# Semaphores of a stage cleared inside the next stage, one barrier at each seam, last attention stores awaited where they are loaded

## The reference

```
xn = layernorm(x)
s  = attention0(xn)              # 16 heads of 16, full softmax, output projection, + b_o + xn
g  = silu(ffn0(xn))              # router, 8 experts of rank 64, cumulative sums over tokens, two branches
x  = x + s * g
xn = layernorm(x)
s  = attention1(xn)              # same heads, |i - j| <= 64 only, output projection, + b_out
g  = silu(ffn1(xn))              # base matrix + 8 gated LoRA experts of rank 16
x  = x + s * g
```

## Time and profile before

| | us |
|---|---|
| median of three runs | 2464.88 |
| the profiled execution, its own time | 2465.71 |
| its span (first to last instruction) | 2464.1 |
| outside of the span | 1.6 |
| PE busy | 2221.7 (90%) |
| DVE busy | 1840.2 (75%) |
| ACT busy | 1448.4 (59%) |
| POOL busy | 462.4 (19%) |
| mean granted TensorE clock, share of full | 0.948 |

### The profile page before, as it was taken

How to read it: one execution, slowest core, us unless ns; L and a number is a source line. 1 busy time by engine, 2 the same in 40 slices (tenths; PEclk the granted TensorE clock), 3 DMA queues, 4 the chain that set the end, 5 groups by cost and what they waited for, 6 DMA issues and landing times. The chain is left out here.

```text
span 2464.1 us, 44375 instructions
## 1 busy us (share of the span) xinstructions
PE 2221.7 (90%) x14912; PEld 1240.2 (50%) x14912; DVE 1840.2 (75%) x3240; ACT 1448.4 (59%) x2165; POOL 462.4 (19%) x673
## 2 busy tenths in 40 slices
PE   7786899999999999999999999987999986899988
PEld 4564333333333333333333333326888875666688
DVE  5553889999999999999999999922443466798746
ACT  4443177777777777777777777771222222375643
POOL 0000000000000000000000000003555520365645
PEclk8998599999999999999999999999999999597999
DMA  6776700220500500502304002006567459766564
GB/s 208 260 246 191 94 4 6 40 29 3 63 6 8 61 3 12 57 5 32 36 6 56 13 5 63 3 5 173 153 181 167 121 211 361 152 151 138 146 166 129
DMA packets 189121, 231.80 MB, mean 94 GB/s; under 512 B 72720, under 2 KB 122768, under 8 KB 186064
## 3 DMA queue, kind: packets, MB, share of 16 engines
q1 hardware_dynamic: 176048, 210.46, 35.0%
q10 hardware_dynamic: 7184, 14.10, 2.7%
q0 software_dynamic: 5728, 5.00, 0.9%
HBM read 138.97 MB, written 89.13 MB: 93 GB/s over the span
## 5 line engine op out<-in xcount | busy, mean ns | idle before, releaser
L1018 DVE TENSOR_REDUCE a_maxes<-a_ps_a 128x2 f32<-128x1024 f32 x1024 | 1202.2, 1221 | 115.4 <-PE a_ps_a L1139 111.6
L1083 ACT ACTIVATE a_prob<-a_ps_s 128x512 f32<-128x512 f32 (+1 forms) x1376 | 1035.7, 804 | 351.2 <-PE a_ps_s L1165 345.2
L1165 PE MATMUL a_ps_s<-a_Q,a_K 50*128 50x512 f32 x2048 | 594.7, 454 | 89.3 <-ACT a_prob L1083 89.1
L1139 PE MATMUL a_ps_a<-a_K,a_Q 48*128 48x512 f32 x2048 | 552.5, 456 | 26.1 <-DMA a_Q<-s_halves 14.6
L1177 PE MATMUL a_ps_o<-a_prob,a_V 128*17 128x512 f32 x4096 | 542.6, 602 | 0.1
L1165 PEld LDWEIGHTS a_ps_s<-a_Q,a_K 50*128 50x128 f32 x2048 | 278.2, 186 | 505.6 <-ACT a_prob L1083 455.7
L1139 PEld LDWEIGHTS a_ps_a<-a_K,a_Q 48*128 48x128 f32 x2048 | 246.6, 190 | 231.5 <-issue 108.8
L976 POOL DMA_DIRECT2D a_Q<-a_m_parts x128 | 64.3, 503 | 1288.1 <-DVE a_m_parts L1010 1281.3
L1585 DVE CUSTOM_DVE_ANT_0 a_scratch<-a_ps_a,k_mask 128x256 f32<-128x256 f32 (+1 forms) x512 | 178.0, 410 | 34.5 <-PE a_ps_a L1702 32.2
L1645 ACT ACTIVATE a_prob<-a_ps_s 128x512 f32<-128x512 f32 (+1 forms) x256 | 135.3, 583 | 104.2 <-PE a_ps_s L1738 103.0
L1177 PEld LDWEIGHTS a_ps_o<-a_prob,a_V 128*17 128x17 f32 x4096 | 68.2, 95 | 150.1 <-issue 99.7
(11 more groups left out here) (196 smaller groups left out, 2284.7 us busy)
## 6 DMA issues: line engine op xcount, KB each, us to landing
s_halves<-p_parts SPq DMA_DIRECT2D x32, 512.0 KB, 4.8
s_halves<-k_K SPq DMA_DIRECT2D x32, 512.0 KB, 7.5
a_Q<-s_halves SPq DMA_DIRECT2D x186, 64.0 KB, 10.3
a_K<-s_halves SPq DMA_DIRECT2D x42, 256.0 KB, 9.3
s_xT<-p_xT SPq DMA_DIRECT2D x32, 256.0 KB, 3.8
s_cT<-p_cT SPq DMA_DIRECT2D x32, 256.0 KB, 3.6
k_wb<-s_w SPq DMA_DIRECT2D x16, 512.0 KB, 7.8
c_wb<-s_w SPq DMA_DIRECT2D x16, 512.0 KB, 7.2
```

What stands on the lines that cost most here:

```text
L1018: nc.vector.tensor_reduce(maxes[:, :, slot, qt, kc], ps_a[:, o:o + 2 * CH].rearrange("p (z k) -> p z k", z=2), AX.X, ALU.max).then_inc(a_d ...
L1083: nc.scalar.activation(prob[:, ring:ring + len(t), :].rearrange("p r q -> p (r q)"), ps_s[:, bank:bank + len(t) * CH], ACT.Exp, scale=scal ...
L1139: last = nc.tensor.matmul(ps_a[:, o + side * CH:o + (side + 1) * CH], Q[rows, q0:q0 + P], K[rows, k0:k0 + CH], start=True, stop=True)
L1165: last = nc.tensor.matmul(ps_s[:, bank + x * CH:bank + (x + 1) * CH], K[rows, k0:k0 + P], Q[rows, q0:q0 + CH], start=True, stop=True)
```

## The change

A list `W["retired"]` collects the semaphores of a stage when the stage ends. Nothing is cleared there and no second barrier is made. The next stage takes other semaphores from the pool, and its POOL stream ends with a call of `clear_retired`, which clears those of the stage before (they may be two ranges, then there are two pairs of DRAIN and clear). k1, k2 and k3 keep the old way. The waits for the last `s_att` stores are moved from the end of a0 and a1 into SP's stream of c0 and c1; for that the tile `o_out` and its semaphores live longer than the stage.

```diff
+def clear_retired(nc, W):
+    if W["retired"]:
+        nc.clear_and_free_semaphores(W["retired"])
+        W["retired"].clear()
 class Names:
-    def __init__(self, nc, ctx, tag):
-        self.nc, self.ctx, self.tag = nc, ctx, tag
+    def __init__(self, nc, ctx, tag, retired=None):
+        self.nc, self.ctx, self.tag, self.retired = nc, ctx, tag, retired
     def release(self):
-        if self.sems:
+        if self.retired is not None:
+            self.retired.extend(self.sems)
+        elif self.sems:
             self.nc.clear_and_free_semaphores(self.sems)
             self.nc.all_engine_barrier()
# all seven stages: Names(nc, ctx, tag, W["retired"]), and as the last thing of their POOL stream
+            clear_retired(nc, W)
# phase_attend_full: o_out and o_stored come from X, which outlives the stage
-            pool.wait_ge(o_stored, DMA * (NIT + 2))
+            clear_retired(nc, W)
# phase_attend_band, sync: o_out and o_stored come from KQ
-            for b in range(2):
-                wait_apart(sp, o_stored[b], DMA * NCH * NG // 2, passed)
# phase_combine_experts, sync, loop over c
                     wait_apart(sp, m_ready, TT * c, passed)
+                    if c == 1:
+                        wait_apart(sp, X["o_stored"], DMA * (NIT + 2), passed)
                     load_attention(c)
# phase_combine_lora, sync, loop over c
                     load_turned_rows(c + BUFS)
+                    if c == 0:
+                        for b in range(2):
+                            wait_apart(sp, KQ["o_stored"][b], DMA * NCH * NG // 2, passed)
                     load_attention(c + BUFS)
# the end of the program
         phase_combine_lora(nc, W, S, KQ, S["x1"], out)
+        clear_retired(nc, W)
```

More of the change, by code:

```diff
@@ L107, in phase_weights @@
     with ExitStack() as ctx:
-        n = Names(nc, ctx, "w")
+        n = Names(nc, ctx, "w", W["retired"])
         square = {k: n.sb(k, [P, DK, D]) for k in ("WQ", "WK", "WinvT", "W1T", "WOT", "WIQ", "WIK")}
@@ L386, in phase_project @@
     with ExitStack() as ctx:
-        n = Names(nc, ctx, f"p{layer}")
+        n = Names(nc, ctx, f"p{layer}", W["retired"])
         xn = L["xn"]
@@ L885, in phase_attend_full @@
     with ExitStack() as ctx:
-        n = Names(nc, ctx, "a0")
+        n = Names(nc, ctx, "a0", W["retired"])
         K = n.sb("K", [P, 2 * LONG], F32R)
@@ L895, in phase_attend_full @@
         recip = n.sb("recip", [P, TT, G])
-        o_out = n.sb("o_out", [P, TT, G, C])
+        o_out = X["o_out"]
         WAT = 4
@@ L928, in phase_attend_full @@
         o_done = n.sem("o_done")
-        o_stored = n.sem("o_stored")
+        o_stored = X["o_stored"]
         out_clear = n.sem("out_clear")
@@ L1285, in band_buffers @@
     KQ = {"K": n.sb("K", [P, BAND_BUFS * BAND_LONG], F32R), "Q": n.sb("Q", [P, BAND_BUFS * BAND_LONG], F32R),
+          "o_out": n.sb("o_out", [P, 2, TT, G, C]), "o_stored": [n.sem(f"o_stored{b}") for b in range(2)],
           "early": n.sem("early"), "loaded": [n.sem(f"loaded{b}") for b in range(BAND_BUFS)],
@@ L1445, in phase_attend_band @@
     with ExitStack() as ctx:
-        n = Names(nc, ctx, "a1")
+        n = Names(nc, ctx, "a1", W["retired"])
         K, Q, kq_early, kq_loaded = (KQ[name] for name in ("K", "Q", "early", "loaded"))
@@ L1455, in phase_attend_band @@
         recip = n.sb("recip", [P, 2, TT, G])
-        o_out = n.sb("o_out", [P, 2, TT, G, C])
+        o_out = KQ["o_out"]
         ps_s = n.ps("ps_s", BANKS * CH)
@@ L1479, in phase_attend_band @@
         o_clear = n.sem("o_clear")
-        o_stored = [n.sem(f"o_stored{b}") for b in range(2)]
+        o_stored = KQ["o_stored"]
         block = ctx.enter_context(nc.Block())
@@ L1841, in phase_combine_experts @@
     with ExitStack() as ctx:
-        n_ = Names(nc, ctx, "c0")
+        n_ = Names(nc, ctx, "c0", W["retired"])
         x_io = n_.sb("x_io", [P, 2, TT, D])
@@ L2169, in phase_combine_lora @@
     with ExitStack() as ctx:
-        n_ = Names(nc, ctx, "c1")
+        n_ = Names(nc, ctx, "c1", W["retired"])
         BUFS = LORA_BUFS
@@ L2428, in recurrent_blocks @@
             "ident": n.sb("ident", [P, P]), "mask": n.sb("mask", [P, WIN]),
-            "ones": n.sb("ones", [P, P]), "half": n.sb("half", [P, TT]),
+            "ones": n.sb("ones", [P, P]), "half": n.sb("half", [P, TT]), "retired": [],
         }
@@ L2442, in recurrent_blocks @@
         X = {"wb": n2.sb("wb", [P, HALF_FT, CH]), "kt_loaded": n2.sem("kt_loaded"),
+             "o_out": n2.sb("o_out", [P, TT, G, C]), "o_stored": n2.sem("o_stored"),
              "wb_loaded": n2.sem("wb_loaded")}
```

## The result

The changed kernel takes 2450.24 us (median of 20 runs, 2443.59 to 2461.85), the kernel before beside it 2458.62 us (20 runs, 2450.34 to 2476.41). The ratio is 0.9959 with a 95% interval of 0.9943 to 0.9975: about 10 us less, between 6 and 14. I had forecast 2459.7 us, 6.0 us less, with "within 0.5%" at 0.86. The sign was right, and the gain was larger than forecast. The 2459.7 us had started from one profiled execution at 2465.71 us, which lies 7.1 us above the kernel before's median of 20 runs.

The account below looks back on a forecast made before the run. PE, DVE or transfers set the pace inside stages, so only block ends change: 1.65 + 0 + 0.05 + 2.15 + 2.15 = 6.0 us off the profiled 2465.71 us gives 2459.7 us, range 2450 to 2465 us.

Parts of the forecast that it names:

- the end of a0: Seam a0 to c0: POOL's DRAIN keeps its 3.49 us but starts directly behind the last store; 2.15 us earned.
- the bounds 0.2 and 5.6: At a0's end: 0.2 us earned if POOL's DRAIN ends at 1676.0 regardless, 5.6 us if it is short.
- POOL's DRAIN is short: Rival at a0's end: the DRAIN is as short as others, 9.45 us earned in all, 2456.3 us; chance 0.04.
- the clock's gains: Rival: low-clock stretches at a1's end and a0's start shrink, 3.5 and 4.1 us more, 2456.2 or 2452 us; chance 0.12.
- The price of a second barrier: At the block ends: 0.55 us for each second barrier removed; 1.65 us at w, p0 and c0 together.
- In a1 the 1.6 us of SP's wait: End of a1: SP's whole 1.6 us wait for the last store earned, with 0.55 us of barrier, 2.15 us.
- the end of the program: Behind c1: one barrier fewer but one DRAIN and clear more, 0.05 us earned.
- p1: Seam p1 to a1: 0 earned, as PE's later wait for a transfer grows by the half microsecond saved.
- The clock: PE's granted clock around the seams: it falls before the change could matter, so nothing was counted.
- a DRAIN that ends when it did: Rival at a0's end: POOL's DRAIN still ends at 1676.0; 4.05 us earned in all, 2461.7 us; chance 0.27.
- The cases at 9.45 us and beyond: Rivals with larger gains: short POOL DRAIN at a0's end (chance 0.04) and shrinking low-clock stretches (chance 0.12).
- its slower neighbour: Rival at a0's end: POOL's DRAIN ends as before; 4.05 us earned instead of 6.0, 2461.7 us; chance 0.27.

Follow-up runs that it names:

- experiment 1: Kernel before with only the wait for a0's last stores moved from POOL to SP's stream of c0: 2457.99 us, ratio 0.9977.
- run 9: Kernel before with a plain DRAIN added on POOL at a0's end, behind the wait for the stores, ahead of the jump; PE idle 8.08 us there.
- run 12: Kernel before with the clear of one spare semaphore added on POOL at a0's end, behind the wait for the stores; PE idle 4.86 us there.
- run 13: Kernel of experiment 2 with a plain DRAIN added between the wait and the clear of a0; PE idle 7.67 us there.
- experiment 2: Changed kernel with both waits for the last attention stores put back at the ends of a0 and a1: 2453.64 us, ratio 0.9956.
- experiment 3: Kernel before with only the wait for a1's last stores moved into SP's stream of c1: 2458.16 us, ratio 1.0003.

## Why the prediction was wrong

**The step that failed** is the size of one term, "the end of a0". I took 2.15 us between the bounds 0.2 and 5.6; it measured 5.64, the far bound, which as the rival "POOL's DRAIN is short" had a chance of 0.04. The term left the DRAIN at a0's end the 3.49 us that it had before. My reason was that the only row of this kind has 3.49 us from its own start, and that the changed kernel puts a DRAIN directly behind the store. Both are true, and experiment 1 even gives the 6.26 us that follow. What I missed stands in the order in front of the prediction: the DRAIN that comes first in the changed kernel is the one of line 66, not the barrier's. I treated the two as one sort of instruction. The runs show that they aren't. At the same place in the kernel before, a plain one took 3495 ns (run 9) and a clear's 64 (run 12); in the changed kernel with its waits put back, 3500 (run 13) and 95 (experiment 2). By the seams, 1.6 us of the 5.64 are the wait (4.15 us in experiment 2, 2.52 with it moved), 0.55 the barrier, and the remaining 3.5 us the DRAIN that I had kept. The row of line 88 could not decide it: all ten DRAINs there are short, but each stands behind a plain one that had paid. It was a reason to leave the question open between the bounds, not to choose. Why a clear's DRAIN is short stays open.

**The starting point.** Of the 9.5 us between the forecast 2459.7 and the median 2450.24, 7.1 us are the execution that I subtracted from: 2465.71 us, where 20 runs of the kernel before have a median of 2458.62. Only 2.4 us are the difference of the medians (8.4 us) against my 6.0. A sum of 10.5 us taken from the same 2465.71 ends at 2455.2. So the time stands at the lower edge of my range, 2450 us, for another reason than the clock's gains for which I had drawn the edge there.

**Shown right.** The price of a second barrier, 0.55 us: 0.55, 0.6 and 0.6 us at w, p0 and c0. The clears in p0, c0, p1 and a1 hide; the one in a0 stands behind the store and costs its 0.2 us (199 ns), and those of c1's semaphores at the program's end can't hide. The new waits in c0 and c1 cost nothing. In a1 the 1.6 us of SP's wait were all earned (experiment 3: 4.49 to 2.86), and what is late next is the issue of the store, until 2345.22, with SP's DRAIN at 2345.3; with the barrier the gap fell by 2.5 us where I had 2.15. What the surplus is stays open. Without the barrier the seam was 0.9 to 1.0 us shorter here (2.86 to 1.97, and 4.49 to 3.46 in experiment 2), not 0.55, but before the change the gap itself lies between 4.12 and 4.96 us.

**Too small: the end of the program.** 0.6 us instead of 0.05. I charged a DRAIN and a clear at 0.25 each on top of a barrier. Clears in a row without a barrier cost less than that, and the third barrier of before was a slow one (the longest of ten, 0.9 us).

**Not to be decided: p1.** Behind p1 PE's wait for the transfer was to grow by the barrier's half microsecond. It was 7.89 us before and 7.83 after, as these rows of the changed kernel show:

```profile
2085.07 1.19 PE L1713 MATMUL a_ps_a<-k_K,k_Q 48*128 48x192 f32 x6 [12.73 <-PEq L396]
...
2115.26 0.53 PE L1749 MATMUL a_ps_s<-k_Q,k_K 50*128 50x192 f32 x1 [7.83 <-DMA k_K<-k_ones]
```

but over the runs of both kernels that wait lies between 3.5 and 8.4 us, so half a microsecond can't be seen in it.

**The clock.** I counted nothing for it, and no seam's gap decided it. In the changed kernel the clock still falls at a1's end, with a gap of 1.97 us:

```profile
2343.00:2346.00 3.00, 0.69 (x5) 0.48 (x5) 0.68 (x2) 0.29 (x1) 0.00 (x0) 0.86 0.26 60
2346.00:2354.00 8.00, 7.73 (x42) 7.50 (x42) 2.25 (x10) 1.21 (x5) 0.00 (x0) 0.62 0.94 210
```

PE was idle for less than half as long as before and still ran the next microseconds at a mean of 0.62, that is for the most part at the lower level, 0.50 or 1.2 GHz. The reading that I had drawn from the Trainium skill (TensorE: Matmul & The Clock Gate, section "Why this matters for your kernels"), that a gap of half the length might not cost the clock, isn't borne out by this seam.

**The rule that I weighed.** The Trainium skill (PSUM — Partial Sum Buffer, section "Engine vs sequencer instructions") has a DRAIN wait until its engine is fully idle. For computing the trace agrees, a clear's DRAIN included: in p0 one starts at 187.4 us beside POOL's last computing, which ends at 188.30, and takes 1025 ns, until 188.4. The rival that I drew from it, a DRAIN that ends when it did, gave 8.2 us in experiment 1 and was measured at 6.26. Two DRAINs at the same place with 64 and 3495 ns show that "idle" isn't one state that both of them wait for.

**The chances.** The cases at 9.45 us and beyond had 0.16 between them and the forecast with its slower neighbour 0.73. With the bounds of 0.2 and 5.6 us that I had, and one row to choose by, that was too sure.

## What to carry to other kernels

At a seam, look up by line which instruction is the long one, and which *kind* it is, before assuming that another instruction of the same name inherits its length; when the changed kernel puts a different one first, give both lengths a real chance. If a GpSimd stage that issues many transfers ends in a long DRAIN, put a semaphore clear behind the last transfer, or hide a plain DRAIN ahead of it while GpSimd waits anyway. A second barrier of all engines was worth 0.55 to 0.6 us at the three seams where it could be read alone, and a wait for a store at a stage's end was worth its whole length, where the issue of the store was what came last.

## What the runs showed of the hardware

- A plain DRAIN on GpSimd behind 162 of its own transfers took 3.49 us in six runs (3492, 3492, 3492, 3495, 3500, and 4344 with the store's issue in it), whether the last had landed or not, and 3.41 behind 161, when the last store was SP's. A DRAIN that belongs to a semaphore clear took 0.06 to 0.1 us in its place, or 0.88 with the store's issue in it, and a plain DRAIN right behind the clear 0.04 to 0.05. Why, and whether the price grows with the number of transfers, stays open: behind one landed store a plain DRAIN took 0.14 us, and behind one not landed, with two clears ahead of that store, it ended 1.7 us behind the end of the issue.
- One barrier of all five engines with its clear cost SP 0.53 us in the mean of ten, the longest 0.9; two clears in a row at the changed kernel's end took 0.4 us together.
- The same program differs by 10 us and more from run to run, in step with the mean granted clock: 12 runs of the changed kernel go from 2438.48 us at 0.959 to 2457.45 us at 0.949.
